# Graph layer and recurrent layer on one core: the edge search batch by batch, and 18 low halves of the lines by TensorE and ScalarE

## The chip, the cores and the metric

The kernel runs on one core of a Trainium2 chip (trn2). The metric is the time of one execution on the device, in microseconds (us). The engines are called as in the profile: PE is TensorE, DVE is VectorE, ACT is ScalarE, POOL is GpSimd and SP is SyncE. ACT, SP and POOL also issue DMA transfers from their own queues.

## The reference, cut to what matters

```python
def gnn(x, src, dst, weight, bias):            # 3125 nodes, 53125 edges sorted by dst, 256 channels
    h = x @ weight + bias
    agg = segment_sum(h[src], dst, 3125)
    deg = maximum(segment_sum(ones, dst, 3125), 1)
    return agg / deg[:, None]

def lstm(x, U, V, b):                           # 3125 steps in sequence, hidden size 256
    # c_new = h * c + i * g ;  h_new = o * tanh(c_new)

x = x + gnn(layernorm(x), src, dst, W, b)
x = x + lstm(layernorm(x)[None], ...)[0]
```

## The kernel before, in words

**Layout.** The 3125 nodes are 125 chunks of 25 steps. Node 25c + t lies on partition c, and the kernel works on 25 blocks of 125 nodes, one for each step t. The recurrence is run for all chunks at once, several rounds over the steps, so that starting states converge.

**Start.** Everything the change touches lies in the first 85 us. It has three strands.

*The lines.* A line is a row h of one node, as two float16 parts: a high part and a low part (what the high part left over), 514 numbers. For block j, DVE takes statistics of x (`chunk_stats`, L1390, then L1395 and L1354), ACT takes a root (`deviation`, L766), and DVE makes the inverse root with one Newton step (`chunk_deviation`, L1407 to L1412), for five blocks at a time. ACT normalises a block (`first_norm`, L772), PE transposes it (L1083, two transposes), ACT copies the high part (L822) and DVE the low part (`zT_low`, L1510). PE multiplies by the weights (L1094 for the bias, L1097 for six products). ACT copies the high part of the result (L827), DVE subtracts it to give the low part (L1531, `line_ready`). This is a pipeline over steps j with a few blocks in flight; a step of it here always means one value of j.

*The edge search.* Edges are handled in 625 tiles of up to 128 edges (called windows in the code), five batches of 125. DVE compares rows of dst with thresholds (L1371, five instructions), PE sums them (L1031, 25 products), DVE turns the sum into row numbers (L1381, L1382), POOL fetches those rows with five indirect DMAs (L610), DVE finds the start in the row (`window_starts`, L1452 to L1460), POOL fetches the edges with five indirect DMAs (L617), waits for all of them and casts them (L623, `edges_f`). DVE computes a chunk number and a key for all 640 columns at once (`edge_places`, L1466 to L1479, in steps 13 and 14), PE transposes them (`turn_keys`, L1055, ten transposes, in step 15) and ACT copies them to float16 (`copy_keys`, L781 to L786, `keys_ready`).

*The comparisons and counts.* For each group of four tiles DVE compares the keys with an iota (`one_hots`, L1489, called the hots; 157 groups), PE multiplies them, four products (`count`, L1067, `count_ps`), and ACT copies the counts out (`counts_out`, L799, `counted`). Hots sit in a ring of six buffers. The first batch (32 groups) has to be counted before the sums can begin. DVE makes two groups in each step from step 17, and the rest behind the last line; there PE adds three products of no use for each group (`keep_busy`, L1074).

**Main loop.** A list of 650 places w written out by hand follows: in each, PE does one product of counts for a later batch and two of the sums (L1113, L1115), and at fixed places DVE finishes a block (`finish`, L1552 to L1561), POOL takes its root (`root`, L657 to L661), DVE normalises it (L1582), PE transposes it (`turn_z2`, L1123) and multiplies by U (`gates_x`, L1144). Early steps of the recurrence are woven in. At w = 2 and w = 14 DVE takes maxima over U and V (L1374, 1536 columns each), for which POOL has halved the weights (`halve`, L628). SP loads those weights once `edges_f` is set (L533 to L536). After the list come the last 41 steps of the recurrence, in two halves of the columns (L1236 on PE).

**Order.** Each engine runs its own instruction list in order, and waits are on semaphores. PE's list for step j is: transposes of j, products of block j - 2, (keys), counts of the groups whose hots were made in step j - 1. ACT's is: normalise j + 1, high part of zT j, high part of line j - 2, (keys), counts out.

```python
            for k in range(first_hots(BLOCKS + 1).start, OUTS):      # ACT, behind the lines
                counts_out(min(HOT_WINDOWS * (k + 1), WINDOWS) - 1)
```
```python
                    if s == 0:                                       # PE, first sums of a block
                        if t % RUN == 0:
                            pe.wait_ge(counted, (t // RUN + 1) * OUTS)
                        if t == 0:
                            pe.wait_ge(line_ready, BLOCKS)
```

## Time and profile before

| | |
|---|---|
| median of 3 runs | 496.7 us (495.86 to 497.5) |
| profiled execution | 495.42 us, span 493.6 us |
| mean granted PE clock | 0.989 |
| busy: PE, DVE, ACT, POOL | 85%, 74%, 70%, 35% of the span |
| first product of the sums (main loop) | 84.47 us from the span's start |

The span runs from the first to the last instruction; the profiled execution took 1.8 us more than its span. Busy shares are averages over three stages (start, main loop, recurrence) with different limits, so the start is read on its own, by the chain of waits and by the order of instructions in time. Where an instruction follows another without a gap, its duration overlaps with the next one's, and the distance of the starts is what the engine spends on it.

### The profile page before, as it was taken

The numbers are of one execution on the slowest core, as the hardware profiler recorded it, in microseconds if no ns is written. First come the engines' busy times: TensorE is split into PE (matmuls) and PEld (weight loads), VectorE is DVE, ScalarE is ACT, GpSimd is POOL, SyncE is SP. The second block draws the span as 40 slices with busy tenths as digits, with TensorE's granted clock in tenths as the row PEclk, the third lists the DMA queues.
The fourth block names the chain that finished last, engine by engine and source line by source line (L and its number), as shares of the span: only waits on it lengthen the run. The fifth ranks groups of instructions, "written<-read, shape, count | busy, mean of one in ns | idle before, by whom it ended". The sixth has DMA issues, their size and how long they took to land.

```text
span 493.6 us, 15382 instructions
## 1 busy us (share of the span) xinstructions
PE 420.1 (85%) x6094; PEld 365.6 (74%) x6094; DVE 363.4 (74%) x1157; ACT 345.9 (70%) x894; POOL 173.5 (35%) x313
## 2 busy tenths in 40 slices
PE   2487799978899999999999899997677878999992
PEld 2265577867788888888888788876577777888881
DVE  3869799987788677686776833535577778888884
ACT  1346598456877776777775764556799999999991
POOL 4442600154337345354544523421122222222220
PEclk9999899999999999999999999999999999999996
DMA  8524002320010001000100000000000000110111
GB/s 194 132 52 131 0 2 72 104 90 1 4 51 1 1 1 55 1 1 1 53 2 3 1 22 33 2 1 30 26 3 5 3 3 3 58 35 23 56 56 59
DMA packets 9604, 16.91 MB, mean 34 GB/s; under 512 B 2006, under 2 KB 7451, under 8 KB 9526
## 3 DMA queue, kind: packets, MB, share of 16 engines
q1 hardware_dynamic: 7922, 13.32, 8.7%
q10 hardware_dynamic: 724, 1.67, 1.5%
q0 software_dynamic: 880, 0.86, 0.8%
q8 instruction: 50, 0.82, 0.7%
q14 instruction: 28, 0.23, 0.1%
HBM read 6.23 MB, written 9.61 MB: 32 GB/s over the span
## 4 chain that ended last, share of the span: by engine, by line
DVE 40%; PE 34%; ACT 10%; issue 8%; POOL 6%; DMA 1%; SPq 0%; DVEq 0%; ACTq 0%
PE bank L1144 10%; DVE hots L1489 8%; PE bank L1113 7%; PE bank L1115 7%; ACT tc L946 5%; DVE h L1702 5%; DVE h L1739 5%; DVE c_st L1697 4%; PE bank L1169 3%; DVE h_flat L1702 3%; POOL rstd L658 3%; PE bank L1067 3%; POOL newton L657 2%; PE bank L1097 2%; DVE x_sb L1555 2%
## 5 line engine op out<-in xcount | busy, mean ns | idle before, releaser
L1067 PE MATMUL bank<-hots 128*128 128x125 f16 x625 | 120.6, 220 | 0.2 <-DVE hots L1489 0.2
L1489 DVE TENSOR_TENSOR hots<-iota,kp 128x1024 f16<-128x1024 f16 x157 | 105.6, 701 | 20.0 <-PE bank L1067 17.0
L1236 PE MATMUL bank<-h,V 128*128 128x62 f16 (+1 forms) x2952 | 102.7, 192 | 18.6 <-DVE h L1702 11.1
L1236 PEld LDWEIGHTS bank<-h,V 128*128 128x128 f16 x2952 | 94.9, 97 | 29.6 <-issue 28.0
L1113 PE MATMUL bank<-h_flat,counts 125*128 125x257 f16 x375 | 97.3, 273 | 0.2 <-ACT counts L799 0.2
L1115 PE MATMUL bank<-h_flat,counts 125*128 125x256 f16 x375 | 96.4, 271 | 0.0
L657 POOL TENSOR_SCALAR newton<-rstd,var_eps 125x1 f32<-125x1 f32 x48 | 33.6, 701 | 116.9 <-DVE rstd L1561 114.5
L799 ACT ACTIVATE counts<-bank 125x500 f16<-125x500 f32 x96 | 55.4, 607 | 20.5 <-PE bank L1067 19.0
L1113 PE MATMUL bank<-h_flat,gx 125*128 125x257 f16 x250 | 68.2, 273 | 0.0
L691 POOL TENSOR_TENSOR hc<-h_flat,c_st 128x126 f32<-128x126 f32 x80 | 34.1, 426 | 96.6 <-DVE c_st L1697 91.7
L1115 PE MATMUL bank<-h_flat,gx 125*128 125x256 f16 x250 | 67.4, 270 | 0.0
L1067 PEld LDWEIGHTS bank<-hots 128*128 128x128 f16 x625 | 56.5, 97 | 8.7 <-DVE hots L1489 1.0
L844 ACT ACTIVATE gx<-bank,gb,gx_scale 128x250 f32<-128x250 f32 (+1 forms) x84 | 40.5, 534 | 28.8 <-PE bank L1144 28.8
L1144 PE MATMUL bank<-z2T,U 128*128 128x250 f16 (+1 forms) x504 | 55.7, 259 | 5.7 <-DVE z2T L1587 4.9
L799 ACT ACTIVATE gx<-bank 125x500 f16<-125x500 f32 x64 | 37.7, 592 | 21.5 <-PE bank L1067 19.3
L1144 PEld LDWEIGHTS bank<-z2T,U 128*128 128x128 f16 x504 | 43.5, 97 | 12.3 <-DVE z2T L1587 7.5
L1113 PEld LDWEIGHTS bank<-h_flat,counts 125*128 125x128 f16 x375 | 36.6, 98 | 4.6 <-ACT counts L799 0.4
L932 ACT ACTIVATE gate<-bank,w_unscale 128x252 f32<-128x252 f32 x82 | 38.5, 470 | 0.4 <-PE bank L1236 0.4
L1702 DVE SCALAR_TENSOR_TENSOR h<-gate,tc 128x126 f16<-128x126 f32 (+1 forms) x80 | 23.5, 294 | 20.7 <-ACT tc L946 20.7
L1115 PEld LDWEIGHTS bank<-h_flat,counts 125*128 125x128 f16 x375 | 36.6, 98 | 1.5
L1169 PE MATMUL bank<-h,V 128*128 128x125 f16 x348 | 27.7, 219 | 10.8 <-ACT bank L862 8.4
L869 ACT ACTIVATE gate<-bank,w_unscale 128x500 f32<-128x500 f32 (+1 forms) x48 | 27.6, 575 | 10.9 <-PE bank L1169 10.3
(171 smaller groups left out, 795.1 us busy)
## 6 DMA issues: line engine op xcount, KB each, us to landing
h_dram<-h_flat SPq DMA_DIRECT2D x1, 3137.2 KB
x_dram<-x_sb SPq DMA_DIRECT2D x5, 625.0 KB
out_dram<-x_sb SPq DMA_DIRECT2D x4, 560.0 KB
x_sb<-in_x_dram SPq DMA_DIRECT2D x3, 560.0 KB
x_sb<-in_x_dram ACTq DMA_DIRECT2D x2, 560.0 KB
out_dram<-x_sb SPq DMA_DIRECT2D x1, 336.0 KB
out_dram<-x_sb SPq DMA_DIRECT2D x4, 65.0 KB
gx<-in_L_gnn_weight_dram ACTq DMA_DIRECT2D x1, 256.0 KB, 3.8
```

The costliest lines, as they stand in the source:

```text
L657: link(nc.gpsimd.tensor_scalar(t, y, v, y, ALU.mult, ALU.mult))
L799: nc.scalar.activation(counts[g % 2][:, :, :, n0:n0 + n], ps_count[group % 3][0:NB, 0:n * KEYS].rearrange("p (n r t) -> p r t n", n=n, r=RUN),
L844: nc.scalar.activation(gx[:, at:at + n, m, :], gates_bank(tile // 2)[:, half * TB * NB:half * TB * NB + n * NB].rearrange("p (s k) -> p s ...
L932: nc.scalar.activation(gate[:, q, 0:2 * HH, 0:n], ps_g[q][:, 0:2 * HH * n].rearrange("p (m k) -> p m k", k=n), ACT.Tanh, scale=w_unscale[: ...
L1067: nc.tensor.matmul(ps_count[group % 3][:, pos * KEYS:(pos + 1) * KEYS], hots[:, ring, 0, g // 2, :, g % 2], hots[:, ring, 1, g // 2, 0:KEY ...
L1113: nc.tensor.matmul(ps_sum[turn % 2][:, 0:D + 1], of, line[:, s, D:2 * D + 1], start=(s == 0), stop=False, skip_group_check=True)
L1115: return nc.tensor.matmul(ps_sum[turn % 2][:, 0:D], of, line[:, s, 0:D], start=False, stop=(s == BLOCKS - 1), skip_group_check=True)
L1144: mm = nc.tensor.matmul(gates_bank(at_unit)[:, half * TB * NB:half * TB * NB + n_blocks * NB], U16[:, w_part, d, m * P:(m + 1) * P], z2T[: ...
L1169: mm = nc.tensor.matmul(ps_early[:, (m - m0) * CHUNKS:(m - m0 + 1) * CHUNKS], V16[:, v_part, d, m * P:(m + 1) * P], h16[:, h_part, d, :], ...
L1236: mm = nc.tensor.matmul(to[:, (m - m0) * n:(m - m0 + 1) * n], V16[:, v_part, d, m * P:(m + 1) * P], h16[:, h_part, d, c0:c1], start=False, ...
L1489: nc.vector.tensor_tensor(hots[:, k % RING, :, :, :, :].rearrange("p a h n g -> p (a h) n g"), iota[:, :, :].unsqueeze(1).to_broadcast(of) ...
L1702: return nc.vector.scalar_tensor_tensor(out=to, in0=gate[:, q, 2 * HH:MT, 0:n], scalar=1.0, in1=tc[:, q, :, 0:n], op0=ALU.add, op1=ALU.mult)
```

## The change

Three edits, all in the start.

*Batches.* A batch of 125 tiles gets its own 32 groups (the last one short), so 160 groups in place of 157. `KEY_ROUNDS` = (0, 1), (1, 3), (3, 5): the starts, the edges, the keys and their transposes are done for batch 0, then 1 and 2, then 3 and 4. Starts come before step 0 and in steps 1 and 2 of DVE's list, keys in steps 3, 6 and 8, PE's transposes and ACT's copies in steps 5, 8 and 10. POOL's cast of the edges is gone: DVE reads the integers. Hots start in step 7 (two groups a step, to step 22), counts three steps later (steps 10 to 25), and nothing of batch 0 is left behind the lines; `keep_busy` is gone. PE's products of the comparison with dst run as each of the five comparisons is done, but behind all of POOL's constants (11 now, among them a fill of 32 x 1280 and a 125 x 125 product with -1).

*Low parts.* For blocks 0 to 8 and every even one after (18 of 25), PE subtracts the high part from the result in its bank, by a product with minus the identity, and ACT copies what is left (`line_low`). DVE keeps the seven odd ones from 9 on.

*Roots.* Groups (0, 5), (5, 10), (10, 25) in place of five of five. The bias is split by one ACT and one DVE instruction in place of five of DVE.

The order within a step is also new: PE counts before its subtraction and products; ACT copies low part, then high part, behind the counts. SP's weight loads wait for all edges in place of POOL's cast; the fill of `counts[1]` moved from POOL's first place behind the last line.

```diff
+    NORMS = [(0, 5), (5, 10), (10, 25)]
+    B_LOW = 32
+    CONSTS = 11
+        KEY_ROUNDS = [(0, 1), (1, 3), (3, 5)]
...
-        KEYS_FROM, TURN_KEYS, HOTS_FROM = 13, 15, 17
+        def low_by_dve(t):
+            return t >= 9 and t % 2 == 1
+        TURN_KEYS = (5, 8, 10)
+        HOTS_FROM, HOTS_LATER = 7, 3
...
+        def first_counts(j):
+            return first_hots(j - HOTS_LATER)
...
-            sp.wait_ge(edges_f, 1)
+            for in_ in win_edges_in:
+                sp.wait_ge(in_, 16)
...
-            nc.gpsimd.memset(counts[1][:, :, :, NB:P], 0.0).then_inc(pads_set, 1)
-            pool.wait_ge(pads_set, 1)
...
+            nc.gpsimd.tensor_scalar(minus_one[:, :], ident[0:NB, 0:NB], -1.0, None, ALU.mult).then_inc(consts, 1)
+            nc.gpsimd.memset(edges_p[96:P, :], -1.0).then_inc(consts, 1)
+            pool.wait_ge(consts, CONSTS)
...
-            for in_ in win_edges_in:
-                pool.wait_ge(in_, 16)
-            nc.gpsimd.tensor_copy(win_edges_f, win_edges.rearrange("p b e a -> p a b e")).then_inc(edges_f, 1)
...
+            pool.wait_ge(edges_ps, len(KEY_ROUNDS))
+            pool.wait_ge(line_ps, BLOCKS)
+            nc.gpsimd.memset(counts[1][:, :, :, NB:P], 0.0).then_inc(pads_set, 1)
```
```diff
@@ ACT
+            for j in range(BLOCKS + 3):
+                if j == 3:
+                    deviation(1)
+                if j == 8:
+                    deviation(2)
+                if j + 1 < BLOCKS:
+                    first_norm(j + 1)
+                if j < BLOCKS:
...
+                if j in TURN_KEYS:
+                    copy_keys(TURN_KEYS.index(j))
+                for k in first_counts(j):
+                    counts_out(windows_of(k + 1) - 1)
+                if 0 <= j - 3 and not low_by_dve(j - 3):
+                    line_low(j - 3)
+                if 0 <= j - 2 < BLOCKS:
+                    line_high(j - 2)
@@ PE
+                for k in first_counts(j):
+                    for w in range(windows_of(k), windows_of(k + 1)):
+                        count(w)
+                t = j - 3
+                if t >= 0 and not low_by_dve(t):
+                    pe.wait_ge(line_hi, t + 1)
+                    nc.tensor.matmul(bank[t % 2][0:NB, 0:D], minus_one[:, :], line[:, t, D:2 * D], start=False,
+                                     stop=True, skip_group_check=True).then_inc(line_left, 1)
-                if w % HOT_WINDOWS == HOT_WINDOWS - 1:
-                    keep_busy(3, bank[6])
@@ DVE
+            for j in range(BLOCKS + 3):
+                if j < BLOCKS:
+                    zT_low(j)
+                if j >= 3 and low_by_dve(j - 3):
+                    line_low(j - 3)
+                if j == 0:
+                    chunk_stats(7, 9)
+                if j == 1:
+                    window_starts(1)
+                    chunk_stats(9, 10)
+                    chunk_to_root(1)
+                if j == 2:
+                    chunk_deviation(1)
+                    window_starts(2)
+                if j == 3:
+                    chunk_stats(10, 12)
+                    edge_places(0)
+                if 4 <= j < 8:
+                    chunk_stats(3 * j, 3 * j + 3)
+                if j == 6:
+                    edge_places(1)
+                if j == 7:
+                    chunk_stats(24, 25)
+                    chunk_to_root(2)
+                if j == 8:
+                    chunk_deviation(2)
+                    edge_places(2)
+                for k in first_hots(j):
+                    one_hots(k)
```

## Rows read from the trace of the kernel before

**Rows 1.** Spans of the cores, whole execution.
```profile
core 0: 493.6 us, clock 0.989
```
**Rows 2.** Chain of waits that ended last, 0 to 130 us: start, us, what.
```profile
7.90 2.81 PE bank L1031 x25
...
21.25 1.64 DVE stats L1390 x5
22.89 0.35 DVE mv L1395 x5
...
56.28 1.29 DVE hots L1489 x2
...
60.54 0.33 DVE gx L1510
60.87 0.33 DVE h_flat L1531
61.20 1.20 DVE hots L1489 x2
...
77.30 7.82 DVE hots L1489 x13
```
**Rows 3.** Timeline of ACT, a step of the lines with two groups, and behind them.
```profile
61.87 0.61 ACT L772 ACTIVATE gx<-x_sb,shift,rstd 125x256 f32<-125x256 f32 x1
62.36 0.39 ACT L822 ACTIVATE gx<-bank 128x250 f16<-128x250 f32 x1
62.62 0.41 ACT L827 ACTIVATE h_flat<-bank 125x256 f16<-125x256 f32 x1
62.89 1.10 ACT L799 ACTIVATE counts<-bank 125x500 f16<-125x500 f32 x2
63.82 0.65 ACT L772 ACTIVATE gx<-x_sb,shift,rstd 125x256 f32<-125x256 f32 x1
...
75.79 8.63 ACT L799 ACTIVATE counts<-bank 125x500 f16<-125x500 f32 x16
```
**Rows 4.** Timeline of PE, an early step's products, a full step, and the first sum.
```profile
33.56 1.54 PE L1097 MATMUL bank<-gx 128*125 128x256 f16 x6
...
61.02 0.41 PE L1083 MATMUL bank<-ident,gx 125*128 125x125 f32 x2
61.35 0.32 PE L1094 MATMUL bank<-b,ones 2*125 2x256 f16 x1
61.60 0.88 PE L1097 MATMUL bank<-gx 128*125 128x256 f16 x6
62.32 0.62 PE L1067 MATMUL bank<-hots 128*128 128x125 f16 x8
62.88 0.40 PE L1083 MATMUL bank<-ident,gx 125*128 125x125 f32 x2
...
84.47 0.28 PE L1113 MATMUL bank<-h_flat,counts 125*128 125x257 f16 x1 [0.21 <-ACT counts L799]
```
**Rows 5.** Timeline of the roots and of the edge search.
```profile
17.61 0.17 DVE L1412 SCALAR_TENSOR_TENSOR shift<-mv,rstd 125x5 f32<-125x5 f32 x1
...
37.94 1.35 POOL L623 CAST gx<-gx 125x1280 f32<-125x1280 int32 x1 [3.15 <-DMA gx<-in_dst_src_dram,gx]
...
49.70 0.83 DVE L1479 SCALAR_TENSOR_TENSOR gx<-gx 125x640 f32<-125x640 f32 x1
```
**Rows 6.** DMA issues, 0 to 90 us: median us from issue to landing.
```profile
gx<-in_dst_src_dram,gx POOLq DMA_INDIRECT x5, 4.1
```
**Rows 7.** Windows of 1 us: busy PE, PEld, DVE, ACT, POOL (instructions), granted clock, DMA.
```profile
50.00:51.00 1.00, 0.00 (x0) 0.03 (x1) 1.00 (x3) 0.00 (x0) 1.00 (x1) 1.00 0.00 0
...
53.00:54.00 1.00, 1.00 (x6) 1.00 (x5) 0.71 (x3) 0.00 (x0) 1.00 (x3) 0.50 0.00 0
```
**Rows 8.** Who PE waited for, 84 to 140 us: us in total, times, longest.
```profile
PE bank L1123 <- DVE z L1582: 3.6, 2, 1.9
```
**Rows 9.** Timeline of DVE, the first block finished in the main loop.
```profile
94.18 0.14 DVE L1552 TENSOR_SCALAR inv<-bank 125x1 f32<-125x1 f32 x1
```

More of the change, by code:

```diff
@@ L477, in early_cols, with lows_dve, lows_act @@
             return slice(0, n), slice(CHUNKS - n, CHUNKS)
-        KEYS_FROM, TURN_KEYS, HOTS_FROM = 13, 15, 17
+        def low_by_dve(t):
+            return t >= 9 and t % 2 == 1
+        def lows_dve(t):
+            return sum(low_by_dve(u) for u in range(t + 1))
+        def lows_act(t):
+            return t + 1 - lows_dve(t)
+        TURN_KEYS = (5, 8, 10)
+        HOTS_FROM, HOTS_LATER = 7, 3
         HOTS_AHEAD = 3
@@ L876, in early_tanh @@
                 nc.scalar.activation(tc_w[:, :, of], c_st[:, c_after(t), :, to], ACT.Tanh, scale=0.5).then_inc(e_tc, 1)
-            for k in range(first_hots(BLOCKS + 1).start, OUTS):
-                counts_out(min(HOT_WINDOWS * (k + 1), WINDOWS) - 1)
             UV_HIGH = (56, 62, 68, 74, 80, 86)
@@ L1069, in count @@
                                  start=True, stop=True).then_inc(count_ps, 1)
-            def keep_busy(n, to):
-                for _ in range(n):
-                    nc.tensor.matmul(to[:, 0:2 * P], iota[:, :, 0], iota[:, :, :].rearrange("p n g -> p (n g)"),
-                                     start=True, stop=True)
-            for j in range(BLOCKS + 2):
+            for j in range(BLOCKS + 3):
                 if j < BLOCKS:
@@ L1099, in _ @@
                     mm.then_inc(line_ps, 1)
[L1100 to L1109 removed]
+                if j in TURN_KEYS:
+                    turn_keys(TURN_KEYS.index(j))
             def sums(turn, s):
@@ L1392, in chunk_to_root, with chunk_stats @@
-            def chunk_to_root(c):
-                for j in range(c * X_CHUNK, (c + 1) * X_CHUNK):
+            def chunk_stats(j0, j1):
+                for j in range(j0, j1):
+                    if j % X_CHUNK == 0:
+                        dve.wait_ge(x_in[j // X_CHUNK], 16 * len(SPLIT))
+                    nc.vector.bn_stats(stats[:, j, :], x_sb[:, j, :]).then_inc(stats_ready, 1)
+            def chunk_to_root(n):
+                j0, j1 = NORMS[n]
+                for j in range(j0, j1):
@@ L1416, in top @@
+                done(nc.vector.tensor_scalar(r, r, -0.5, 1.5, ALU.mult, ALU.add))
+                done(nc.vector.tensor_tensor(y, y, r, ALU.mult))
+                nc.vector.scalar_tensor_tensor(out=shift[:, js], in0=mv[:, js, 0], scalar=-1.0, in1=y,
+                                               op0=ALU.mult, op1=ALU.mult).then_inc(rstd_ready, 1)
+            newtons = 0
             def top(n0, n1, of, times):
@@ new lines, in line_low @@
+            def line_low(t):
+                dve.wait_ge(line_hi, t + 1)
+                nc.vector.tensor_tensor(line[:, t, 0:D], bank[t % 2][0:NB, 0:D], line[:, t, D:2 * D],
+                                        ALU.subtract).then_inc(line_low_dve, 1)
+            for j in range(BLOCKS + 3):
+                if j < BLOCKS:
[11 more added lines that the diff above has]
+                    window_starts(2)
+                if j == 3:
+                    chunk_stats(10, 12)
[10 more added lines that the diff above has]
+                    edge_places(2)
@@ L1540, in _ @@
                 for k in first_hots(j):
                     one_hots(k)
-            for k in range(first_hots(BLOCKS + 3).stop, FIRST_HOTS):
+            for k in range(OUTS, FIRST_HOTS):
                 one_hots(k)
```

358 lines of the change are left out of this document (157 added, 201 removed).

## The prediction

> **What bounds the kernel now.** I read the spans first, then the chain of waits for the first 130 us, then the timelines of the engines around it. The whole is 493.6 us long [rows 1], and the first sum of the main loop runs at 84.47 [rows 4]. Behind it the list of places and the recurrence are left as they were, so the question is how much earlier that product comes, and whether the rest keeps the distance. The chain shows what holds it: the first hots come only at 56.28, because the keys exist no sooner; then steps of 1.86 us in which DVE has no gap (0.33 + 0.33 + 1.20); then 13 more hots in 7.82 us behind the last line [rows 2], while ACT copies 16 groups out in 8.63 us [rows 3]. In those steps ACT needs 1.95 us (0.49 normalise, 0.26 zT, 0.27 high part, 0.93 for two groups; 61.87 to 63.82) [rows 3] and PE 1.86 (0.33 transposes, 0.25 + 0.72 products, 0.56 counts; 61.02 to 62.88) [rows 4]. So three engines are full there, and the change takes work off the one on the chain and puts it on the other two.
>
> **Up to the first roots.** PE's 25 products start at 7.90, behind the last comparison, and take 2.81 us [rows 2]. Running them as comparisons land would hide most, but they now wait for POOL's longer list of constants. Counting POOL's list up, I put its end near 7.3, so I take 0.5 us of gain here; bounds are 0.5 us lost (constants at 8.4) and 2 us gained (all but the last five products hidden). Statistics are drawn into the waits of the weight scale, about 1.1 us more. The first roots stand at 17.78 now (17.61 + 0.17) [rows 5]; I put them at 16.2. The bias split shrinks from five linked DVE instructions to one, but the first starts move ahead of step 0, about equal.
>
> **Steps 0 to 10.** For batch 0 the starts are known near 18.5; POOL is still issuing row fetches until then, and an edge fetch lands in 4.1 us [rows 6], about 23. Batches 3 and 4 land near 31, against the cast that starts at 37.94 [rows 5]. Neither is waited for then: DVE is the slow engine here. Its list from 16.2 to the end of step 8, by the rows: 18 statistics of 0.33 (1.64 for five) = 5.9 and 20 aggregations of 0.07 (0.35 for five) = 1.4 [rows 2]; two roots of six small linked instructions, 0.2 each [rows 5], with their waits 2.7; nine low parts of zT at 0.33 = 3.0 [rows 2]; four hots at 0.60 = 2.4 [rows 2]; split of the weights 1.2; starts 2.8 (14 small ones of 0.2); keys 5.4. The last three are estimates; for the keys the widest instruction took 0.83 us for 640 columns [rows 5], and the work is now 17 instructions of 128 or 256 columns in three rounds, some 0.3 each. Sum 24.8, so 41.0 with no wait. PE still runs at its lower level, 1.54 us for six products of 256 columns against 0.88 later [rows 4], so a step is 0.6 + 0.4 + 1.7 = 2.7 us to step 6, and DVE waits for it some 2 us. The end of DVE's step 8 is then 43 to 44, the third round of keys is ready at 42.5, and PE and ACT stand still for it: ACT waits in step 8 for the variances of 15 blocks, in step 9 for their roots (40 to 41), in step 10 for the transposed keys. ACT begins step 11 at 46.3.
>
> **Steps 11 to 27.** ACT gets one more copy of 125x256 out of a bank, 0.27 us as its twin [rows 3], in odd steps only: 2.22 us there and 1.95 in even ones, mean 2.09. PE gets one product of 256 columns, 0.11 us, with a wait on a semaphore of 0.16: 2.13 and 1.86, mean 2.0. DVE falls to 1.53 and 1.86. So ACT becomes the bound. Steps 11 to 23 are 7 x 2.22 + 6 x 1.95 = 27.2, so 73.5; steps 24 and 25 have no norm, 1.5 each, 76.5; the last line's chain (products, high part, subtraction, low part) is serial, 2.2 us. First sum at 78.7. To this I add 1.0 us for the clock and for ACT and PE waiting for each other: 79.7, a gain of 4.8. The bounds are 77 (DVE never waits before step 8) and 84 (below).
>
> **The clock.** PE did nothing from 50 to 51 and the granted clock was 0.50, its level of 1.2 GHz, at 53 to 54 [rows 7]. In the changed kernel PE stands still in steps 8 to 11, so I expect a fall near 42 and a cost of 1 to 2 steps at 3.6 us for 2.1, partly under ACT's own wait. The Trainium skill (TensorE: Matmul & The Clock Gate, HAM oscillation) says that idle gaps make the clock drop and warns of it where the PE waits for other engines; by it the loss of the useless products at the tail would matter too, and the sum would end on the first rival's value.
>
> **The main loop.** DVE is behind when it starts: the first block is finished from 94.18, 9.7 us after the first sum [rows 9, 4], though its 25 sums are done in 7.0 us (0.28 a place), because the last hots of the start and two maxima (some 3.4 us) are in its way. With 160 groups it has three more hots (1.8 us over the loop), but it ends its start hots at about 75 and can do two or three groups and one maximum before the first sum. PE waits 3.6 us for the first two normalised blocks [rows 8]. I take 1.5 us of them as saved; bounds 0 and 3.5. POOL's halving now runs beside the hots and may take twice as long; it is over by 60 to 65 and needed near 80, so it costs nothing; uncovered it would be the nine us that it takes. The fill of `counts[1]` (0.66 us) is under the first sums.
>
> The sum is 4.8 + 1.5 = 6.3 us off 495.4, the profiled execution: 489.1. That execution lies 1.3 us under the median of 496.7, so the forecast against the median is 490.4, with 487.5 to 493 as its own range.
>
> **The rivals.** *The clock stays low* (0.18): the stalls of steps 8 to 11 and the tail without useless products leave PE at 1.2 GHz for two more stretches of about 3.5 us, where the step is 1.5 us longer or a place 0.28 us longer; two or three us are lost. Time 493. For it: the drop before 53 followed one short stall [rows 7]. Against: from step 11 PE has 2.0 us of work in 2.1.
> *All of it comes* (0.17): DVE never waits for PE before step 8 and 3 us of PE's waits go: first sum at 77.3, a gain of 10, time 486.7.
> *Slower: ACT and PE lock* (0.1). Of each line the high part (ACT), the subtraction (PE), the low part (ACT) and the next product into the same bank (PE) now form a loop between two full engines, where DVE used to take one leg. If neither can run ahead, a step is PE's 2.13 plus a copy that PE must wait for, 0.39, and two hand-overs, some 0.1: 2.6 to 2.8 over 15 steps in place of 2.09. It decides from 2.58 on: there all that is won (6.3, and the 1.0 set aside) is gone. At 2.7, the middle, the time is 490.4 - 1.0 + 15 x 0.61 = 498.6. Against: the copy is the last of ACT's step, and PE has 0.87 us of transposes and counts before it needs it.
> *It does not show* (0.09): the main loop waits for something not moved, say POOL's roots, and takes the gain back within 1.5 us; 496. The normalised blocks that PE waits for [rows 8] hang on those roots, which speaks for it; but a root starts only behind the first sums, and comes earlier with them.
>
> **Numbers.** A measurement of this kernel tells 0.3% (1.5 us) from no change. The forecast has 0.46, the clock 0.18 and all 0.17: faster, 0.81 together. The last rival is no change, 0.09, and the lock slower, 0.10. The range takes in the first three and stops short of the lock: 486 to 495.5.
>
> **What would show it.** Right: first sum at 77 to 82; ACT without gaps in steps 11 to 23 at 1.95 and 2.22; DVE with gaps there; hots first at 37 to 39; L1552's twin less than 9 us behind the first sum. Wrong: steps over 2.4 us; third roots later than 42; granted clock of 0.5 beyond 55 us, or a wait of PE in the main loop for weights.

## The result, and the profile after

| | before | after |
|---|---|---|
| median of 9 runs each | 497.50 us (495.86 to 497.87) | 499.71 us (498.30 to 501.54) |
| profiled execution, span | 495.42, 493.6 | 500.82, 499.0 |
| first sum | 84.47 [rows 4] | 85.15 |
| first finish | 94.18 [rows 9] | 95.20 |
| 25th finish | 340.64 | 343.58 |
| first product of the recurrence's last part | 354.07 | 358.79 |

The ratio is 1.0056, interval 1.0037 to 1.0075: slower by over half a per cent, where 490.4 us and a gain of 1.3% were forecast. (1.0056 is also the ratio of the means, 500.04 and 497.26 us; the medians alone stand at 1.0044.) The profiled execution of after is 0.8 us over its mean and that of before 1.8 us under its own; they are read for where the time goes, not for how much.

The start of the edge search, timeline of PE and of DVE (start, us, engine, line, operation; in brackets the idle time before and what ended it; L1064, L1437 and L1484 answer to L1031, L1407 and L1452 of before):
```profile
8.14 2.82 PE L1064 MATMUL bank<-ones_col,gx 125*125 125x1 f16 x25 [8.14 <-POOL gx L636]
...
16.21 0.19 DVE L1437 RECIPROCAL rstd<-sd 125x5 f32<-125x5 f32 x1 [0.85 <-ACT sd L796]
...
20.27 0.31 DVE L1484 SCALAR_TENSOR_TENSOR gx<-gx,ones 125x85 f32<-125x85 int32 x1 [1.71 <-DMA gx<-in_dst_dram,gx]
...
20.89 0.41 DVE L1544 TENSOR_TENSOR gx<-bank,gx 128x250 f16<-128x250 f32 x1
```
PE begins its 25 products only when POOL's last constant is done, as late as before [rows 2], and DVE, which now has the starts ahead of block 0's low part, stands 1.71 us for the fetched rows. The roots are there at 17.4, not 16.2.

Steps 3 to 11, timeline of ACT (L817 is the high part of a line, L802 the normalisation, L796 the root, L810 the copy of the keys):
```profile
26.82 0.39 ACT L817 ACTIVATE h_flat<-bank 125x256 f16<-125x256 f32 x1 [1.31 <-PE bank L1137]
...
29.63 0.38 ACT L817 ACTIVATE h_flat<-bank 125x256 f16<-125x256 f32 x1 [1.40 <-PE bank L1137]
...
40.85 0.22 ACT L796 ACTIVATE sd<-var_eps 125x15 f32<-125x15 f32 x1 [1.40 <-DVE var_eps L1389]
...
49.91 0.66 ACT L810 ACTIVATE kp<-bank 128x256 f16<-128x256 f32 x2 [2.39 <-PE bank L1093]
...
51.91 0.64 ACT L802 ACTIVATE gx<-x_sb,shift,rstd 125x256 f32<-125x256 f32 x1
```
and the same stretch on PE (PEld is its weight load), with its last early step:
```profile
24.44 0.47 PE L1122 MATMUL bank<-h_flat,minus_one 125*125 125x256 f16 x1
24.84 0.47 PE L1134 MATMUL bank<-b,ones 33*125 33x256 f16 x1
25.24 1.54 PE L1137 MATMUL bank<-gx 128*125 128x256 f16 x6
26.57 0.62 PE L1113 MATMUL bank<-ident,gx 125*128 125x125 f32 x2
27.25 0.18 PEld L1122 LDWEIGHTS bank<-h_flat,minus_one 125*125 125x125 f16 x1 [0.45 <-ACT h_flat L817]
27.26 0.47 PE L1122 MATMUL bank<-h_flat,minus_one 125*125 125x256 f16 x1
...
46.13 0.62 PE L1113 MATMUL bank<-ident,gx 125*128 125x125 f32 x2
46.55 1.05 PE L1103 MATMUL bank<-hots 128*128 128x125 f16 x8
47.40 0.41 PE L1122 MATMUL bank<-h_flat,minus_one 125*125 125x256 f16 x1
47.74 0.47 PE L1134 MATMUL bank<-b,ones 33*125 33x256 f16 x1
48.14 1.29 PE L1137 MATMUL bank<-gx 128*125 128x256 f16 x6
49.27 0.60 PE L1093 MATMUL bank<-ident,gx 128*128 128x128 f32 x4
```
A step lasts 2.82 us (24.44 to 27.26): 0.40 for the subtraction, 0.40 for the bias, 1.33 for six products, 0.69 for the transposes. PE's busy column is nearly full in it, but PE is not: in each step up to the one at 44 us the weight load of the subtraction stands 0.45 us or more for ACT's high part, which itself starts when the six products end (26.78) and ends at 27.21. So products, high part and subtraction form a ring, and the ring is the step. At 48.14 the products still need 1.13 us for six; before, they had come down to 0.88 from 35.59 on. PE turns the third keys at 49.27 though DVE had finished them at 46.5: they stand in PE's list behind counts, subtraction and products. And DVE had them late for one more reason, POOL's halving of the weights, which runs from 42.83 to 51.30 (timelines of DVE and POOL; the same instruction of the second round of keys, and then of the third):
```profile
36.56 0.29 DVE L1503 TENSOR_SCALAR gx<-gx 125x256 f32<-125x256 f32 x1
...
44.53 3.36 POOL L655 TENSOR_SCALAR gx<-gx 128x512 f32<-128x512 f32 x2
44.84 0.58 DVE L1503 TENSOR_SCALAR gx<-gx 125x256 f32<-125x256 f32 x1
```
The third round took DVE 2.64 us where the second, of the same shapes, took 1.96. ACT begins step 11 at 51.91, 5.6 us later than forecast.

From there the forecast's step holds: ACT has no gap, and the 13 steps to 79.28 take 27.37 us (27.2 forecast). The tail and the head of the main loop on DVE:
```profile
80.42 0.41 DVE L1550 TENSOR_TENSOR h_flat<-bank,h_flat 125x256 f16<-125x256 f32 x1
83.17 0.42 DVE L1550 TENSOR_TENSOR h_flat<-bank,h_flat 125x256 f16<-125x256 f32 x1 [2.34 <-ACT h_flat L817]
83.52 2.50 DVE L1519 TENSOR_TENSOR hots<-iota,kp 128x1024 f16<-128x1024 f16 x4
...
85.93 1.75 DVE L1407 TENSOR_REDUCE w_max<-gx 128x1 f32<-128x1536 f32 x1
87.59 1.89 DVE L1519 TENSOR_TENSOR hots<-iota,kp 128x1024 f16<-128x1024 f16 x3
89.40 1.75 DVE L1407 TENSOR_REDUCE w_max<-gx 128x1 f32<-128x1536 f32 x1
...
95.20 0.14 DVE L1592 TENSOR_SCALAR inv<-bank 125x1 f32<-125x1 f32 x1
```
DVE waits 2.34 us for the high part of line 23, and the hots of the main loop and both maxima stand behind that wait. The first finish is 10.05 us behind the first sum; it was 9.71.

Two differences follow behind it. The distance to the 25th finish was 246.46 and is 248.38; the last of them, after and then before:
```profile
343.58 0.16 DVE L1592 TENSOR_SCALAR inv<-bank 125x1 f32<-125x1 f32 x1 [0.54 <-PE bank L1147]
```
```profile
340.64 0.16 DVE L1552 TENSOR_SCALAR inv<-bank 125x1 f32<-125x1 f32 x1 [0.54 <-PE bank L1115]
```
And from there to the recurrence's last part it is 15.21 us in place of 13.43, in a stretch with the granted clock at its lower level. Windows of 5 us, after (busy PE, PEld, DVE, ACT, POOL, then the granted clock, DMA share, GB/s):
```profile
345.00:350.00 5.00, 1.92 (x26) 1.51 (x26) 3.60 (x16) 3.06 (x8) 0.71 (x1) 0.94 0.30 107
350.00:355.00 5.00, 4.47 (x44) 4.51 (x45) 1.91 (x4) 1.50 (x4) 0.63 (x1) 0.50 0.07 26
355.00:360.00 5.00, 4.07 (x78) 3.62 (x77) 2.31 (x6) 4.07 (x13) 0.45 (x1) 0.88 0.00 0
```
So the 5.4 us between the two profiled executions are 1.0 to the first finish, 1.9 in the loop, 1.8 at the fall of the clock and 0.7 in the rest. The means differ by 2.8 us, and the other 2.6 are the choice of executions. The first two parts add up to 2.9, close to that 2.8, but one profile of each kernel does not show that it is they. The fall does not come with the change each time: its stretch was 13.4 us long in the profile of before and in four of the experiments, which all hold the change, and 14.8 to 15.2 in the other eleven. Whether the kernel before has it in other executions, no trace shows; 13 of 92 later executions of it had a mean granted clock of 0.988 or 0.989, as the profiled one, and took 495.4 to 496.3 us, the others had a lower one and a median of 497.9. What brings the fall was not found.

### The profile page after: what moved, and what is told of

Read it like the earlier page. It is cut to its first block, busy times and chain, and to the rows that moved or that the text cites. A ratio compares the mean times of both kernels' runs of the same rounds, so it can differ in the third digit from the quotient of the medians.

```text
span 499.0 us, 15440 instructions
## 1 busy us (share of the span) xinstructions
PE 426.7 (86%) x6072; PEld 371.0 (74%) x6072; DVE 360.4 (72%) x1139; ACT 350.6 (70%) x910; POOL 177.0 (35%) x315
## 4 chain that ended last, share of the span: by engine, by line
PE 36%; DVE 31%; ACT 14%; issue 8%; POOL 8%; DMA 2%; DVEq 0%; ACTq 0%; POOLq 0%
PE bank L1176 10%; PE bank L1145 6%; PE bank L1147 6%; ACT tc L979 5%; DVE h L1742 5%; DVE h L1779 4%; DVE hots L1519 4%; DVE c_st L1737 4%; PE bank L1137 3%; PE bank L1201 3%; POOL newton L689 3%; DVE h_flat L1742 3%; PE bank L1103 3%; POOL rstd L690 2%; ACT h_flat L817 2%
## 5 line engine op out<-in xcount | busy, mean ns | idle before, releaser
L1519 DVE TENSOR_TENSOR hots<-iota,kp 128x1024 f16<-128x1024 f16 x160 | 108.5, 703 | 18.0 <-PE bank L1103 17.2
L834 ACT ACTIVATE counts<-bank 125x500 f16<-125x500 f32 x96 | 59.0, 679 | 20.9 <-PE bank L1103 19.4
L689 POOL TENSOR_SCALAR newton<-rstd,var_eps 125x1 f32<-125x1 f32 x48 | 35.9, 747 | 90.7 <-DVE rstd L1601 88.4
L1176 PE MATMUL bank<-z2T,U 128*128 128x250 f16 (+1 forms) x504 | 57.0, 263 | 6.8 <-DVE z2T L1627 6.0
L1176 PEld LDWEIGHTS bank<-z2T,U 128*128 128x128 f16 x504 | 44.7, 100 | 13.7 <-DVE z2T L1627 8.9
L1201 PE MATMUL bank<-h,V 128*128 128x125 f16 x348 | 29.2, 227 | 10.0 <-ACT bank L897 7.8
```

Source lines behind the costliest of these rows:

```text
L689: link(nc.gpsimd.tensor_scalar(t, y, v, y, ALU.mult, ALU.mult))
L834: nc.scalar.activation(counts[g % 2][:, :, :, n0:n0 + n], ps_count[group % 3][0:NB, 0:n * KEYS].rearrange("p (n r t) -> p r t n", n=n, r=RUN),
L1176: mm = nc.tensor.matmul(gates_bank(at_unit)[:, half * TB * NB:half * TB * NB + n_blocks * NB], U16[:, w_part, d, m * P:(m + 1) * P], z2T[: ...
L1201: mm = nc.tensor.matmul(ps_early[:, (m - m0) * CHUNKS:(m - m0 + 1) * CHUNKS], V16[:, v_part, d, m * P:(m + 1) * P], h16[:, h_part, d, :], ...
L1519: nc.vector.tensor_tensor(hots[:, k % RING, :, :, :, :].rearrange("p a h n g -> p (a h) n g"), iota[:, :, :].unsqueeze(1).to_broadcast(of) ...
```

## The experiments

All start from the changed kernel, and each has its ratio to executions of the kernel before that were taken beside it. Each profile shows one execution, and the milestones move between profiles of kernels whose early steps are the same: step 11 from 50.93 to 52.61, the first sum from 84.21 to 85.79 (the changed kernel, e5_tail, e14_place, e15_short_hots). So a gain under 1.7 us in a single profile proves little by itself. Nor do the ratios settle it for one edit alone: the intervals of e3_fill, e4_starts_later, e5_tail and e6_consts all overlap with the changed kernel's, and that of e6_consts is as low as e3_fill's though its first sum came later. The kernels with several edits are the firmer ground. The milestones, in us:

| kernel | ratio to before | step 11 | first sum | first finish | to the 25th |
|---|---|---|---|---|---|
| changed | 1.0056 (1.0037 to 1.0075) | 51.91 | 85.15 | 95.20 | 248.38 |
| e1_low_dve | 1.0139 (1.0119 to 1.0160) | 55.16 | 87.78 | 98.03 | 248.38 |
| e2_first_low_dve | 1.0125 (1.0105 to 1.0144) | 55.58 | 88.53 | 98.58 | 248.47 |
| e3_fill | 1.0024 (1.0000 to 1.0048) | 49.34 | 82.52 | 92.57 | 248.38 |
| e4_starts_later | 1.0019 (1.0000 to 1.0039) | 50.37 | 83.60 | 93.65 | 248.48 |
| e5_tail | 1.0016 (0.9992 to 1.0040) | 50.93 | 84.21 | 91.73 | 248.50 |
| e6_consts | 1.0025 (1.0002 to 1.0048) | 51.81 | 85.90 | 95.94 | 248.44 |
| e9_roots | 1.0082 (1.0053 to 1.0112) | 49.93 | 85.11 | 95.15 | 248.44 |
| e10_table | 1.0056 (1.0029 to 1.0083) | 52.52 | 86.64 | 96.68 | 248.38 |
| e7_all | 0.9948 (0.9929 to 0.9966) | 49.44 | 83.61 | 91.14 | 248.45 |
| e13_hots_later | 1.0009 (0.9992 to 1.0026) | 49.70 | 84.78 | 92.31 | 248.44 |
| e14_place | 1.0050 (1.0033 to 1.0068) | 52.41 | 85.65 | 95.57 | 247.56 |
| e11_all_roots | 0.9914 (0.9892 to 0.9936) | 46.42 | 82.06 | 89.59 | 248.77 |
| e12_nofill | 0.9988 (0.9966 to 1.0011) | 48.94 | 84.24 | 91.76 | 248.56 |
| e15_short_hots | 1.0069 (1.0039 to 1.0098) | 52.61 | 85.79 | 95.84 | 247.77 |
| e16_best | 0.9898 (0.9866 to 0.9931) | 43.78 | 80.90 | 88.42 | 248.02 |

**Who holds the early steps.** Two kernels give low parts back to DVE, all 18 or only those of blocks 0 to 8.
```diff
         def low_by_dve(t):
-            return t >= 9 and t % 2 == 1
+            return True                        # e1_low_dve
+            return t < 9 or t % 2 == 1         # e2_first_low_dve
```


> All 25 low parts of the lines by DVE, as before the change; PE subtracts nothing and ACT copies no low part. The rest of the change stays. Theory A (the loop between ACT's high part, PE's subtraction and the next products holds steps 3 to 10 at 2.81 us and keeps PE at 1.2 GHz until 49 us): early steps 2.3 us at the low level, 1.2 GHz left before 42 us, ACT begins step 11 at 47 to 49 instead of 51.9, steps 11 to 23 at 1.95, first sum near 79 instead of 83.5, and 3 to 5 us off the time of the changed kernel. Theory B (DVE's own list holds steps 3 to 10, and the subtraction only hides beside it): step 11 begins at 51.9 as now or later, since DVE gets nine low parts more; only the late steps gain, 13 x 0.14 = 1.9 us, or nothing, as DVE is then full again at 1.86.

> Low parts of blocks 0 to 8 by DVE as well, so PE and ACT keep only the eight even ones from 10 on. Theory A: the early gain of the run with all low parts by DVE is here in full (step 11 at 47 to 49), the late steps stay at 1.95 and 2.22; 2 to 4 us off. Theory B: step 11 within 0.5 us of 51.9, no change in the time.

Both are slower than the changed kernel, by 0.8% and 0.7%. Without the subtraction PE's step is 2.29 us where nothing else holds it (22.44 to 24.73), as theory A said, but now PE waits for DVE, which has the statistics and keys of those steps. Timeline of PE, e1_low_dve:
```profile
22.44 0.47 PE L1133 MATMUL bank<-b,ones 33*125 33x256 f16 x1
...
24.73 0.47 PE L1133 MATMUL bank<-b,ones 33*125 33x256 f16 x1
...
27.80 0.44 PE L1133 MATMUL bank<-b,ones 33*125 33x256 f16 x1 [0.72 <-DVE h_flat L1548]
...
38.92 0.36 PE L1133 MATMUL bank<-b,ones 33*125 33x256 f16 x1 [2.00 <-DVE h_flat L1548]
...
43.71 0.44 PE L1133 MATMUL bank<-b,ones 33*125 33x256 f16 x1 [0.94 <-DVE h_flat L1548]
```
So both theories have a part. The ring of ACT and PE does make the early step 0.53 us longer, but the way out of it by DVE costs more than the ring: given DVE's list as it stands, the moved low parts pay, early ones too.

**PE's level.** A product of 256 columns that nobody reads, in each of steps 3 to 10.
```diff
                 t = j - 3
+                if 3 <= j <= 10:
+                    for _ in range(1):
+                        nc.tensor.matmul(bank[4][:, 0:2 * P], iota[:, :, 0], iota[:, :, :].rearrange("p n g -> p (n g)"),
+                                         start=True, stop=True)
```


> The changed kernel with one product of no use (256 columns) in PE's list of each of steps 3 to 10, ahead of the subtraction, where PE waits for ACT. If the low clock in steps 5 to 10 comes of the short gap in each step, PE reaches 2.4 GHz near 38 us instead of 49, steps fall from 2.8 to about 2.0 and step 11 begins 2 to 4 us sooner. If the gap has nothing to do with it, each step is 0 to 0.2 us longer, the clock rises at 49 as now, and the time is the same or 1 us more.

First sum 2.63 us earlier, ratio down by 0.3%, with intervals that overlap. Timeline of PE, e3_fill:
```profile
28.61 1.18 PE L1141 MATMUL bank<-gx 128*125 128x256 f16 x6
29.63 0.38 PE L1113 MATMUL bank<-ident,gx 125*128 125x125 f32 x2
29.85 0.27 PE L1122 MATMUL bank<-iota 128*128 128x256 f16 x1
30.27 0.32 PE L1126 MATMUL bank<-h_flat,minus_one 125*125 125x256 f16 x1
30.52 0.32 PE L1138 MATMUL bank<-b,ones 33*125 33x256 f16 x1
30.77 0.88 PE L1141 MATMUL bank<-gx 128*125 128x256 f16 x6
```
With more work PE is faster: the six products take 0.88 from 30.77 on, where the changed kernel has 1.54 at 30.87 and up to 44.80. A step is then 1.86 us (33.39 to 35.25). The durations of all of PE's products fall, the useful ones too, so the gain comes through the clock. While PE was still slow, the product of no use cost nothing: the step was 2.82 us with it as well, since it fell into the wait for the high part.

One profile could be luck, as the rise moves between executions. But all five kernels with this product have their first group of six products under 1.54 us at 26.23 to 35.83, and the nine without it that keep the early subtractions have it at 44.30 to 53.23. The two without either, e1_low_dve and e2_first_low_dve, have it at 35.83 and 34.08.

**The wait for the fetched rows.** The starts of batch 0 go behind block 0's low part.
```diff
             split_weights()
-            window_starts(0)
...
                 if j == 0:
+                    window_starts(0)
                     chunk_stats(7, 9)
```


> DVE makes the starts of batch 0 behind the low part of block 0's zT instead of ahead of it, so that zT does not wait for the row fetch that lands at 20.25. If that wait carries through (theory C): the first products of block 0 start near 19.7 instead of 22.0, step 11 1 to 2 us sooner, and 1 to 2 us off the time. If the edge batches set the pace of steps 6 to 10, step 11 begins at 51.9 as now and the time is unchanged.

The wait of 1.71 us is gone, the first sum comes 1.55 earlier, and the ratio is 0.4% lower. Two others try to bring the fetch or the roots forward. In the first, PE's 25 products wait for seven constants of eleven (POOL finishes seven before it starts the other four; PE waits for all behind these products, and POOL still makes all of them ahead of the row fetch). In the second, ACT takes its first root before it copies the weights.
```diff
-            pool.wait_ge(consts, 2)
+            pool.wait_ge(consts, 7)
-            pe.wait_ge(consts, CONSTS)         # ahead of the 25 products
+            pe.wait_ge(consts, 7)
...
+            pe.wait_ge(consts, CONSTS)         # behind them
             turn_tops(0, 1, bank[4], 1)
```


> PE's 25 products of the edge search wait for seven constants, not for all eleven (POOL's product with -1 and its three larger fills come after). If the constants hold them (theory E): products start at 5.3 to 5.5 and end at 8.3 to 8.4 instead of 10.98, row numbers 2.5 us sooner, first roots 1.5 to 2.5 us sooner. Whether the time follows tells what the row fetch waits for: if it waits for the fetch's own issue, step 2 starts 2 us sooner and the time falls by 1 to 2 us; if the landing at 20.25 is set by the loads of x ahead of it, the landing stays at 20 and the time is the same.

```diff
+            deviation(0)                       # e10_table
             act.wait_ge(scales_ready, 1)
...
-            deviation(0)
             first_norm(0)
```


> ACT takes the first root ahead of its copies of the weights, as before the change. In the trace of the changed kernel a second table load of 1.28 us stands between the variances (15.1) and the root (15.97). Expected: one table load, at 5.4; first root near 15.2; first roots ready 0.8 us sooner. As DVE then waits for the row fetch to 20.27, the time is the same (0 to 0.3 us off) if that wait comes last, and 0.8 us less if it does not.

Neither moves the first sum forward. In e6_consts the row numbers are known 1.6 us earlier (9.43 for 11.00), but DVE has the rows at 20.08 for 20.25. In e10_table the second load of ScalarE's tables is gone; in the changed kernel it stands ahead of the root (timeline of ACT):
```profile
14.67 1.28 ACT L796 ACT_TABLE_LOAD   x1
15.97 0.21 ACT L796 ACTIVATE sd<-var_eps 125x5 f32<-125x5 f32 x1
```
The root came at 15.20 and the inverse 0.5 us earlier, since the root now waited for the variances, and DVE then stood longer for the rows (2.36 us for 1.71).

**The tail.** Hots 32 to 34 in steps 23 and 24, the maxima in steps 24 and 25.
```diff
                 for k in first_hots(j):
                     one_hots(k)
+                if j == BLOCKS - 2:
+                    one_hots(OUTS)
+                    one_hots(OUTS + 1)
+                if j == BLOCKS - 1:
+                    one_hots(OUTS + 2)
+                    dve.wait_ge(halved, 7)
+                    extreme(1, U_sb[:, :, :, :].rearrange("p d n h -> p (d n h)"))
+                if j == BLOCKS:
+                    extreme(2, V_sb[:, :, :, :].rearrange("p d n h -> p (d n h)"))
-            for k in range(OUTS, FIRST_HOTS):
-                one_hots(k)
...
-            weights_work = {2: lambda: uv_extreme(1, U_sb),
-                            14: lambda: uv_extreme(2, V_sb),
-                            15: lambda: largest(1, 3),
+            weights_work = {15: lambda: largest(1, 3),
```


> DVE makes the three hots ahead (groups 32 to 34) in steps 23 and 24, not behind the low part of line 23 in step 26, and takes the two maxima over U and V in steps 24 and 25, where it now waits 2.3 us for ACT. Theory D (DVE's queue behind that low part and the two maxima sets the start of the main loop): the first sum follows ACT's last low part at once, near 83.7 instead of 85.15, the first block is finished by DVE some 7.3 us behind the first sum, at 91 instead of 95.2, and the time falls by 3 to 4 us. Rival: PE's sums and POOL's roots set it; the first block is finished earlier but the second and third are not, and the time falls by less than 1 us.

Timeline of DVE, e5_tail:
```profile
79.72 0.68 DVE L1519 TENSOR_TENSOR hots<-iota,kp 128x1024 f16<-128x1024 f16 x1
80.32 3.40 DVE L1407 TENSOR_REDUCE w_max<-gx 128x1 f32<-128x1536 f32 x2
83.64 0.41 DVE L1550 TENSOR_TENSOR h_flat<-bank,h_flat 125x256 f16<-125x256 f32 x1
```
The maxima now fill the 2.34 us that DVE had stood, at the price of 0.33 us for the first sum, and the first finish is 7.5 us behind the first sum, not 10.05.

**The burst of the third roots.** The group (10, 25) is cut in two, so that the statistics of blocks 15 to 24 move from steps 5 to 7 into steps 9 to 12. ACT takes the third root in step 6 and the fourth in step 13.
```diff
-    NORMS = [(0, 5), (5, 10), (10, 25)]
+    NORMS = [(0, 5), (5, 10), (10, 15), (15, 25)]
...
+                if 9 <= j < 13:
+                    chunk_stats((15, 17, 20, 22)[j - 9], (17, 20, 22, 25)[j - 9])
+                if j == 12:
+                    chunk_to_root(3)
+                if j == 13:
+                    chunk_deviation(3)
```


> Roots in four groups, (0, 5), (5, 10), (10, 15), (15, 25), with the last ten statistics in DVE's steps 9 to 12, where it has room. Theory F (the burst of statistics, aggregations and the root of 15 blocks in DVE's steps 4 to 8 makes PE and ACT stand still): roots of blocks 10 to 14 near 37 instead of 43.9, step 11 begins at 47 to 49 instead of 51.9, and 2.5 to 4 us off the time. Rival: the keys' rounds and PE's order at the low clock set step 10 whatever the roots do: step 11 within 1 us of 51.9, 0 to 1 us off.

Step 11 began 2 us earlier, and step 13 stood for the fourth roots: the first sum was where it had been. Cut alone it gains nothing.

**Together.** Product of no use, later starts, tail, seven constants and the early root in one kernel; then with hots later; then with the roots cut.

> Five edits together: the useless product in steps 3 to 10, the window starts of batch 0 behind the low parts of line 0, one-hots 32 to 34 and both maxima inside steps 23 to 25, the first 25 products waiting for seven constants, ScalarE's first root ahead of the weight copies. Theory A (several stalls, each on the path to the first sum or behind it, so that the gains add): first sum at 80 to 82 us (85.15 in the changed kernel, less 2.6 for the product and 1.5 for the starts), first finish 7.5 us behind it at 88 to 89.5, 248.4 us to the 25th finish, time 493 to 496, ratio 0.991 to 0.997. Rival B (the steps have one holder, and each edit alone had already taken it away): first sum 82.5 or later, as in the best single edit, ratio 0.998 to 1.003.

> The five edits, and the one-hots of the first groups given out later in the steps (from step 8 on, two at first, where the changed kernel begins at step 7 with three). Theory (VectorE's list up to the third keys ends the early stretch, so one-hots moved behind it pay): the step-11 normalisation 0.8 to 1.5 us earlier than with the five edits alone, the first sum by as much. Rival (TensorE at its low level holds those steps, VectorE has room): the same step-11 time within 0.3 us, and a later first finish where the one-hots now lie behind line_low(23).

> The five edits and the third group of roots cut in two, so that VectorE's statistics for tiles 15 to 24 move from ahead of step 8 to steps 9 to 13. Theory (with the low level and the fetch wait taken away, VectorE's list up to the third keys is what is late): step 11 begins 1 to 2 us earlier than with the five edits alone, first sum 79 to 80.5, ratio 0.988 to 0.995. Rival (as when cut alone, the burst only moves and step 13 waits for the fourth roots): the stretch from step 11 on shows a stall of 2 us or more, first sum not earlier, ratio as with the five edits or up to 0.003 above.

```diff
-        HOTS_FROM, HOTS_LATER = 7, 3
+        HOTS_FROM, HOTS_LATER = 8, 2           # e13_hots_later
```
(Both kernels make two hots a step. The 3 that became 2 is the number of steps from the hots to their counts, so that the counts stay where they were, from step 10 on.)

The five edits give 494.71 us, faster than before (0.9948), and 1.1% under the changed kernel; each alone had given 0.4% at most. The first sum came at 83.61 and not at 80 to 82: the level rose early, in the products at 29.01, and fell again before 41.55 (1.54 for six products), so that this profile shows one gain and not both. Later hots are worse (1.0009): step 11 did not come earlier, the rival's figure. With the roots cut as well the kernel takes 492.93 us (0.9914), step 11 begins at 46.42, and a new stall shows (timeline of ACT, e11_all_roots):
```profile
46.42 0.64 ACT L802 ACTIVATE gx<-x_sb,shift,rstd 125x256 f32<-125x256 f32 x1
...
52.61 0.21 ACT L796 ACTIVATE sd<-var_eps 125x10 f32<-125x10 f32 x1 [1.79 <-DVE var_eps L1396]
```
So DVE's list up to the third keys does hold step 11, once the rest is out of the way. Not all of the 3.0 us against e7_all are its length: here the level stayed up (0.88 from 37.97 on), and the third round of keys was done by 40.51, as POOL's halving began at 40.39, and took 1.97 us, not 2.48 as in e7_all. Taking the product of no use out again tells its share in this company.

> The six edits without the product of no use in steps 3 to 10. Theory (TensorE's low level costs a step its length on its own, also with VectorE's list shortened): step 11 begins 1.5 to 3 us later than 46.4, granted clock 0.50 until 45 us or later, first sum 83.5 to 85, ratio 0.994 to 0.998. Rival (VectorE's list alone held those steps, the product only looked like a gain): step 11 within 0.5 us of 46.4, ratio 0.990 to 0.993.

Step 11 is 2.5 us and the first sum 2.2 us later, the ratio 0.7% higher, and six products take 1.54 us until 42.16 where e11_all_roots has 0.88 from 37.97. The two intervals (0.9892 to 0.9936 and 0.9966 to 1.0011) lie apart, so the gain by the level is in the time too. So both holders are real, and each hides part of the other.

**The main loop.** Two kernels ask where the 1.9 us come from. A group of one tile costs DVE a full comparison of four; e15 compares two tiles' places.
```diff
-                group, pos, _ = out_group(w + WINDOWS)                 # e14_place
+                group, pos, _ = out_group(w + 1 + WINDOWS)
+                if w == 0:
+                    one_hots(FIRST_HOTS)
```
```diff
+                if windows_of(k + 1) - windows_of(k) < HOT_WINDOWS:    # e15_short_hots
+                    nc.vector.tensor_tensor(hots[:, k % RING, :, 0, :, :],
+                                            iota[:, :, :].unsqueeze(1).to_broadcast([P, 2, P, 2]),
+                                            kp[:, k, :, 0:2].unsqueeze(2).to_broadcast([P, 2, P, 2]),
+                                            ALU.is_equal).then_inc(hot_ready, 1)
+                    return
```


> The changed kernel with each group's one-hots in the main loop issued one place earlier in VectorE's list, their number unchanged. If the +1.92 us between the first and the 25th finish comes from where the one-hots stand against the finishes, this brings it from 248.4 back to 246.5 to 247 and the ratio to 1.001 to 1.003. If it is the work of the three more one-hots alone, the stretch stays at 248.2 to 248.6 and the ratio at 1.005 to 1.007.

> The changed kernel, and in the five groups that hold one tile only (the last of each batch) the comparison is made over two tiles' places in place of four, 512 numbers a partition for 1024. Theory A (the 1.9 us are the work of three more one-hots): about 0.33 us less for each of the four short groups in the loop, so 247.0 to 247.3 us from the first to the 25th finish (248.4 in the changed kernel, 246.5 before), ratio 1.002 to 1.004. Rival B (they come from the copies and waits around a group, not from VectorE's work): 248.2 to 248.5, ratio 1.005 to 1.007.

The stretch fell to 247.56 and 247.77, each between its two theories, and neither ratio shows a gain. (A short comparison took 0.42 us for 0.69, so four of them in the loop are 1.1 us less of DVE's work, for 0.6 us less of time.) Who PE waited for from 84 to 360 us, in total, times and longest, after:
```profile
PE bank L1176 <- DVE z2T L1627: 6.0, 9, 1.5
PE bank L1155 <- DVE z L1622: 4.8, 2, 2.6
```
and before:
```profile
PE bank L1144 <- DVE z2T L1587: 4.9, 7, 1.5
PE bank L1123 <- DVE z L1582: 3.6, 2, 1.9
```
PE waits for DVE 2.3 us more at these two lines, which is enough for the loss of 1.9; it is read from one profile of each. The loss is complete at the 15th finish; over the last ten blocks the two kernels keep the same pace to 0.04 us. What share the number of the hots has, and what share their places against the finishes, stays open.

**The best of it.** The six edits, the fourth roots one step earlier (statistics in steps 8 to 11) and the short groups.

> The six edits, the fourth roots one step earlier (statistics of tiles 15 to 24 in steps 8 to 11) and the short groups' comparison over two tiles' places. If both sum up: no stall over 1 us between steps 11 and 14 (1.8 with the six edits alone), first sum 80.5 to 81.5, 247.1 us to the 25th finish, time 490 to 491.5, ratio 0.984 to 0.989. Rival (VectorE's list gets longer ahead of the third keys and gives it back): step 11 at 47.5 or later, first sum at 82, ratio 0.989 to 0.992.

492.28 us, ratio 0.9898 (0.9866 to 0.9931), the fastest of all, though against e11_all_roots the intervals overlap. Step 11 came at 43.78, but the stall stayed (1.83 us for the variances), only earlier; the first sum is 1.2 us earlier and the time 0.65.

## Why the prediction was wrong

It forecast 490.4 us and the kernel takes 499.7. The range, and the 0.81 for faster, failed with it.

*Up to the first roots.* Wrong by 1.2 us. POOL's constants end at 8.1, near the worse bound of 8.4, not at 7.3; the 0.5 us did not come. The second table load, 1.28 us, was not in the sum; without it, in e10_table, the roots stood 0.3 us earlier. The first starts were put at 18.5; DVE had the rows at 20.25 and the starts at 20.97. The forecast called the starts moved ahead of step 0 "about equal", without asking what stood behind them if the rows were late. That was the step's own wait, 1.71 us.

*Steps 0 to 10.* This is the step that failed: third keys at 46.5 for 42.5, step 11 at 51.91 for 46.3. The 4.0 us at the keys are three terms. The later start is 1.2. DVE's list is 0.8: from 17.4 to 46.5 are 29.1 us, less 4.7 of waits, so 24.4 of work, where the 24.8 less the two hots of step 8 are 23.6. And the waits are 2.0: 4.7 (1.71 for the rows; 0.20, 0.40 and 2.39 for ACT, itself behind PE) where 2.7 lie between that work and 42.5. Behind the keys come 1.6 us more: the forecast had 3.8 to step 11, and they took 5.4, as the keys waited 2.8 us in PE's list. As to PE, the forecast let it be slow "to step 6"; it was slow to step 9, in steps of 2.82 us that the ring of products, high part and subtraction sets. The forecast feared a fall of the clock from stalls near 42; six products still took 1.54 us at 40.30 and 44.80, so nothing could fall, and what hurt was a level that had not yet risen. e3_fill and e12_nofill show this part at 2.2 to 2.6 us, e4_starts_later the wait for the rows at 1.5, which is within what profiles of one start differ by. Such a fall behind a stall, which the prediction took from the Trainium skill (TensorE: Matmul & The Clock Gate, HAM oscillation), did come in an experiment: in e3_fill PE stood 2.21 us for ACT up to 40.63, and the granted clock of 40 to 45 was 0.79. The section's own case is a PE that waits for DMA; here it waits for ACT.

*POOL's halving.* The forecast feared that it "may take twice as long" beside the hots, and held that it costs nothing. It took 8.5 us, and 8.9 before the change. The price fell on DVE: 0.7 us in the third round of keys and 0.35 in one instruction of the third root (0.52 for 0.17), all of it ahead of the third keys. That covers the 0.8 us by which the list was too short.

*Steps 11 to 27.* Right up to step 23: 27.37 us for 27.2, ACT the bound, DVE with gaps. From there to the first sum are 5.87 us, where 5.2 and 1.0 in reserve were forecast. The rival in which ACT and PE "lock" did not happen here (2.22 and 1.95 to the digit). Its ring is there in the early steps, at the lower level, where no rival had looked for it: 2.82 us against 2.29 without the subtraction.

*The main loop.* Wrong by sign. The forecast let DVE "do two or three groups and one maximum before the first sum". In its list they stand behind `line_low(23)`, which waits for ACT, and were done behind it: the first finish was 10.05 us behind the first sum, not under 9. e5_tail shows 2.5 us of that. The three more hots, "1.8 us over the loop", were counted as hidden; PE waits for DVE in the loop, and 1.9 us or more showed in every kernel with 160 groups whose hots in the loop were as in the changed one.

*The sum.* 4.8 forecast to the first sum, 0.7 lost: 5.5 off. 1.5 forecast in the loop, 1.9 lost and 0.3 more to the first finish: 3.7 off. Together 9.2; between 490.4 and 499.7 are 9.3. That these agree is in part luck: the profiled executions differ by 5.4 us, and the sum leaves out the 1.8 at the fall of the clock and 0.7 in the rest. The slower rival gave 498.6 for a lock over 15 late steps, which did not come; its time was close by chance. Of the signs of being wrong that the forecast named, two came: steps over 2.4 us (2.82) and third roots later than 42 (43.9). None of the rivals held that the early steps keep their length, and the bounds given for them, "77 and 84", stopped short of it.

## What to carry to other kernels

Where work is moved ahead in an engine's list, look for the first semaphore that it brings along and for what stands behind it: here the starts brought a DMA landing, the short wait of one line held hots and maxima, and the keys stood behind products. Look too at which engine's work now falls beside another's: DVE's keys beside POOL's halving were a third longer. Price early products at the level that the rows show for them, and ask how long it lasts when their spacing changes. And an edit that gains nothing alone (the roots) can gain beside others: cut stalls in the order in which they end the step, and run them together.

## What the runs showed of the hardware

*The level of the early products.* Six products of 256 columns took 1.54 us (0.22 from start to start) until 48 us in the changed kernel and 0.88 (0.12) after, while the granted clock of the windows from 20 to 50 read 1.00 throughout. So the durations, about twice apart as 1.2 and 2.4 GHz are, tell the level and that column does not, at the start. Before the change they were down at 35.59. With one product more a step they came down at 26 to 36 in five kernels, without it, the early subtractions kept, at 44 to 53 in nine. With the same list up to step 4 the rise came at 29.01 in e7_all and at 35.83 in e11_all_roots, so it moves between executions. The Trainium skill (TensorE: Matmul & The Clock Gate) says that the clock goes by how busy the PE has been and that the records of it are sometimes not to be trusted; both agree with these rows.

*DVE beside POOL.* While POOL halves weights (a 128x512 float32 instruction takes it 1.5 to 1.75 us), single instructions of DVE last longer: 0.58 for 0.29, 0.67 for 0.28, a comparison 1.10 for 0.68. In the twelve kernels with the change whose third round of keys runs beside the halving, the round took 2.20 to 2.64 us; in the four where the halving began at its very end or later (e11_all_roots, e12_nofill, e13_hots_later, e16_best), 1.97. Neither the product of no use nor the cut roots separates the two sets, but no run moved the halving alone.

*The fetch of rows.* The indirect fetch of rows was issued at 12.25 us in the changed kernel and at 10.68 in e6_consts, and DVE had the rows at 20.25 and 20.08. The loads of x, 560 KB each, run in that time; that they are the cause was not tried.

*A table load.* With weight copies ahead of the first root ACT loads its tables a second time, 1.28 us; with the root first, it does not. The Trainium skill (ScalarE: Activation LUTs, What ACT_TABLE_LOAD costs) gives about 1283 ns, which agrees, and adds some 1380 ns of drain for each switch, of which nothing shows here: the copy ahead of the load ends at 14.65, and the root starts 1.30 us after the load does.
